# Causal attention: probabilities normalised and turned on TensorE instead of scores computed a second time transposed

## What is computed

```python
def _L3_attn_ref(x, Wk, Wq, Wv, Wp, bp):
    B, T, C = x.shape
    H = N_HEADS
    hs = C // H
    k = (x @ Wk).reshape(B, H, T, hs)
    q = (x @ Wq).reshape(B, H, T, hs)
    v = (x @ Wv).reshape(B, H, T, hs)
    scale = C ** (-0.5)
    wei = jnp.einsum('bhtd,bhsd->bhts', q, k) * scale
    mask = jnp.tril(jnp.ones((T, T), dtype=bool))
    wei = jnp.where(mask, wei, -jnp.inf)
    wei = jax.nn.softmax(wei, axis=-1)
    out = jnp.einsum('bhts,bhsd->bhtd', wei, v).reshape(B, T, C)
    return out @ Wp + bp
...
    t = t + _L3_attn_ref(_ln_t(t), L3_attn_Wk, L3_attn_Wq, L3_attn_Wv, L3_attn_Wp, L3_attn_bp)
    t = t + _L3_ffn_ref(_ln_t(t), L3_ffn_gate_w, L3_ffn_gate_b, L3_ffn_w1, L3_ffn_b1, L3_ffn_w2, L3_ffn_b2)
```

## Time and profile before

| | |
|---|---|
| runs of before (us) | 1140.48, 1141.38, 1141.67; median 1141.38 |
| profiled execution: own time, span | 1142.76, 1140.9 |
| PE, DVE, ACT, POOL busy | 91%, 59%, 51%, 45% of the span |
| causal attention's steps | about 765 to 974 us of the span |
| mean granted TensorE clock | 0.958 of full |

### The profile page before, as it was taken

One profiled execution on the slowest core, in us unless ns is written; L12 is line 12 of the kernel. 1 busy time (PEld: TensorE's weight loads), 2 busy tenths in 40 slices (PEclk: granted clock), 3 DMA queues, 4 the chain that ended last, 5 costly groups with the idle time before them and its releaser, 6 DMA issues. The chain is left out here.

```text
span 1140.9 us, 29004 instructions
## 1 busy us (share of the span) xinstructions
PE 1034.0 (91%) x11331; PEld 681.5 (60%) x11331; DVE 668.3 (59%) x1874; ACT 582.7 (51%) x1335; POOL 513.2 (45%) x675
## 2 busy tenths in 40 slices
PE   5999989799979799999999987888888888999998
PEld 2677755477745467776767754554545544466665
DVE  3899834499846456565656653774655556333333
ACT  1676633377633465666666644453444322465553
POOL 4666556487474455554545356242000000364532
PEclk9999999799989899999999997897999997899999
DMA  6500000000000000000000000000000000000000
GB/s 125 96 5 2 2 2 2 1 1 3 1 2 2 1 1 1 2 2 1 1 2 1 2 1 1 2 2 1 1 1 2 1 1 1 1 16 9 9 15 16
DMA packets 28390, 9.72 MB, mean 9 GB/s; under 512 B 26529, under 2 KB 28256, under 8 KB 28256
## 3 DMA queue, kind: packets, MB, share of 16 engines
q1 hardware_dynamic: 25232, 6.95, 2.9%
q10 hardware_dynamic: 3024, 0.92, 0.4%
HBM read 6.29 MB, written 1.57 MB: 7 GB/s over the span
## 5 line engine op out<-in xcount | busy, mean ns | idle before, releaser
L1141 POOL TENSOR_TENSOR fa_e<-fa_e,fa_rc 128x1024 f32<-128x1024 f32 x64 | 120.6, 1895 | 142.2 <-DVE fa_rc L1364 142.2
L1298 ACT ACTIVATE fa_e<-bank,fa_nm 128x256 f32<-128x256 f32 x256 | 118.9, 500 | 0.0
L164 POOL TENSOR_TENSOR ln_v<-MV,eps 128x2 f32<-128x2 f32 (+3 forms) x81 | 16.4, 203 | 162.6 <-DVE MV L201 89.7
L137 PE MATMUL bank<-hT,e_w 96*64 96x512 f32 x384 | 89.4, 600 | 0.0
L2149 ACT ACTIVATE ex_G<-bank,e_b 128x512 f32<-128x512 f32 x96 | 64.5, 687 | 47.3 <-PE bank L137 44.6
L2221 DVE SCALAR_TENSOR_TENSOR X<-bank,ex_L,X 128x96 f32<-128x96 f32 x128 | 31.7, 311 | 91.5 <-PE bank L137 85.0
L1358 DVE TENSOR_REDUCE fa_nm<-bank 128x4 f32<-128x1024 f32 x64 | 75.5, 1220 | 14.5 <-PE bank L1167 14.5
L2052 POOL TENSOR_TENSOR ex_tmp<-e_b,ex_L 128x384 f32<-128x384 f32 x8 | 6.7, 835 | 170.6 <-DVE ex_L L2209 170.6
L1871 ACT ACTIVATE ca_e<-bank 128x768 f32<-128x768 f32 x48 | 38.9, 811 | 82.0 <-PE bank L1680 82.0
L1953 DVE TENSOR_REDUCE ca_z<-bank 128x2 f32<-128x256 f32 x96 | 48.9, 552 | 50.9 <-PE bank L1680 50.9
L137 PEld LDWEIGHTS bank<-e_w,ex_G 128*64 128x64 f32 x1536 | 67.2, 137 | 17.2 <-issue 10.5
(11 more groups left out here) (253 smaller groups left out, 2500.4 us busy)
## 6 DMA issues: line engine op xcount, KB each, us to landing
out_tokens<-X SPq DMA_DIRECT2D x8, 192.0 KB, 2.1
X<-in_x SPq DMA_DIRECT2D x14, 96.0 KB, 3.4
e_w<-in_L_ffn_w SPq DMA_DIRECT2D x2, 576.0 KB
bias0r<-in_L_conv_rpb_table ACTq DMA_DIRECT2D x16, 24.0 KB
m0w<-in_L_conv_mlp_w SPq DMA_DIRECT2D x2, 144.0 KB
m1w<-in_L_conv_w SPq DMA_DIRECT2D x2, 144.0 KB
f_w<-in_L_ffn_W SPq DMA_DIRECT2D x2, 142.5 KB
mixer<-in_mixer SPq DMA_DIRECT2D x1, 256.0 KB
```

The source lines that it names most:

```text
L137: last = pe.matmul(out[columns], weights[:, columns], moving, **flags)
L1141: pool.tensor_tensor(e, e, r.broadcast_to([P, 4, TOK]), ALU.mult).then_inc(s["nrm"], 1)
L1298: last = act.activation(E[v % 4][:, i, c, :], bank[b + i][:, c * TOK:(c + 1) * TOK], ACT.Exp, bias=NM[v % 4][:, i, c:c + 1], accum_out=SU[ ...
```

## The change

Scores are computed once, with the queries on the partitions. The exponential is taken there, image by image and block by block, with the negated maximum as ScalarE's bias and the row sum as its accumulated output. VectorE inverts the sums, GpSimd multiplies the probabilities by them (`probabilities`), TensorE turns the twelve 128x128 blocks of a step in three fills of four (`turn`, into banks 5, 6 and 7), VectorE copies the fills to ET (`turned_out`), and the value product of step c-2 is done in step c. The second pair's scores of a step are issued behind the transposes of the step before. Gone are `shifted`, the transposed mask, `maxima_t`, `shift`, the column of ones, three of the four instructions of `heads_out`, and `keep_warm` in this stage. Half of the projections are copied out by VectorE. The out projection is one block of 48 passes ahead of the first pair's masks in the fifth step of a round. GpSimd normalises in halves of a round, six ahead of the steps and two in them. Two of the residual statistics move behind the last step, and the experts' first token transposes and gate use banks 4 and 5.

```diff
-    UN = 2 * H3
-    UNITS = NG * UN
+    STEPS = NG * H3
     R = TOK * H3
+    FILLS = 3
...
+    NM = [sb(f"nm{i}", [P, NJ, 2]) for i in range(2)]
+    SU = [sb(f"su{i}", [P, NJ, 2]) for i in range(2)]
+    RC = [sb(f"rc{i}", [P, NJ, 2, 1]) for i in range(2)]
     E = [sb(f"e{i}", [P, NJ, 3 * P]) for i in range(2)]
-    T1 = sb("t1", [P, TOK])
-    T2 = sb("t2", [P, TOK])
-    rc = sb("rc", [P, TOK // 32, 1])
+    ET = [sb(f"et{i}", [P, FILLS, 4 * P]) for i in range(2)]
...
+        def probabilities(u, p):
+            pool.wait_ge(s["rec"], 2 * u + p + 1)
+            images = slice(2 * p, 2 * p + 2)
+            for c in range(2):
+                e = E[u % 2][:, images, keys(c)]
+                last = pool.tensor_tensor(e, e, RC[u % 2][:, images, c, :].broadcast_to([P, 2, (c + 1) * P]), ALU.mult)
+            last.then_inc(s["nrm"], 1)
...
+        for m in range(3):
+            for i in range(2):
+                norm(m, i)
+        for u in range(STEPS):
+            for p in range(2):
+                probabilities(u, p)
+            if u in (7, 8):
+                norm(3, u - 7)
+            if u == 15:
+                next(run)
...
+        def scores(u, p):
+
+            n, h = u // H3, u % H3
+            if u == 0:
+                pe.wait_ge(s["abe"], 6)
+                if p:
+                    pe.wait_ge(s["v"], 3)
+            elif h == 0 and p == 0:
+                pe.wait_ge(s["abe"], 6 + 3 * n)
+                pe.wait_ge(s["abd"], 3 * n)
+            after(pe, s["exp"], 2 * (u - 1) + p + 1)
             for c in range(2):
+                for j in range(2 * p, 2 * p + 2):
+                    pe.matmul(bank[j][:, keys(c)], A[n % 2][strip(j, D3), cols(h, c, c + 1)], B[n % 2][strip(j, D3), cols(h, 0, c + 1)],
+                              start=(c == 0), stop=False, skip_group_check=True)
+
+        def masks(p):
+
+            for j in range(2 * p, 2 * p + 2):
+                last = pe.matmul(bank[j][:].rearrange("p (a c) -> p a c", a=2)[:, :, 0:P], k.identb[:],
+                                 k.causal[:, None, :].broadcast_to([P, 2, P]), start=False, stop=True, skip_group_check=True)
+            last.then_inc(s["sc"], 1)
...
+        def turn(u, f):
...
+            pe.wait_ge(s["nrm"], 2 * u + min(f, 1) + 1)
+            landed(u - 1, f)
...
+            if h == 4 and n >= 1:
+                pe.wait_ge(s["oc"], NJ * (n - 1) + f + 2)
+            for b in range(4):
+                j, part = divmod(4 * f + b, 3)
+                last = pe.transpose(bank[5 + f][:, b * P:(b + 1) * P], E[u % 2][:, j, part * P:(part + 1) * P], k.ident[:])
+            last.then_inc(s["et"], 1)
+
+        def landed(u, f):
+
+            if u >= 0:
+                pe.wait_ge(s["ete"], FILLS * u + f + 1)
+
+        def values(u):
...
+            landed(u, FILLS - 1)
+            after(pe, s["ote"], u)
...
+            for q in range(2):
                 for j in range(NJ):
-                    last = pe.matmul(bank[4][strip(j), c * P:TOK], V[n % 2][:, 2 * h + c, j, :], E[step % 2][:, j, 2 * c * P:(c + 2) * P],
-                                     start=(c == 0), stop=(c == 1), skip_group_check=True)
+                    last = pe.matmul(bank[4][strip(j), q * P:TOK], V[n % 2][:, 2 * h + q, j, :], turned[u % 2][:, j, 2 * q * P:(q + 2) * P],
+                                     start=(q == 0), stop=(q == 1), skip_group_check=True)
...
+        for c in range(STEPS + 2):
+            n, h = c // H3, c % H3
+            m, fetch = n + 1, n + 1 < NG
+            if 1 <= c < STEPS:
+                scores(c, 0)
+            if h == 4 and n >= 1:
+                pe.wait_ge(s["ote"], c - 2)
+                for f in range(FILLS):
+                    landed(c - 2, f)
+                if fetch:
+                    pe.wait_ge(s["abe"], 6 + 3 * n + 3)
+                    pe.wait_ge(s["abd"], 3 * n + 3)
+                out(n - 1)
+            if 1 <= c < STEPS:
+                masks(0)
+            after(pe, s["ote"], c - 2)
+            if h == 0 and fetch:
+                if c == 0:
+                    pe.wait_ge(s["v"], 3)
+                tokens(m, 0, 4)
+            elif h >= 3 and fetch:
+                if h == 4 and n >= 1:
+                    pe.wait_ge(s["oc"], NJ * (n - 1) + 1)
+                value_rows(m, h - 3, 4)
+            elif c == STEPS - 5:
+                next(run)
+            if 1 <= c <= STEPS:
+                for f in range(FILLS):
+                    turn(c - 1, f)
+            if c < STEPS:
+                scores(c, 1)
+                masks(1)
+            if h == 0 and fetch:
+                landed(c - 1, 0)
+                tokens(m, 1, 5)
+            elif h == 5 and n >= 1:
+                for half in range(2):
+                    landed(c - 1, 1 + half)
+                    out_t(n - 1, half)
+            elif h in (1, 2, 3) and fetch:
+                for i in range(2):
+                    landed(c - 1, i)
+                    project(m, 2 * (h - 1) + i, 5 + i)
+            elif c == STEPS - 4:
+                landed(c - 1, 0)
+                next(run)
+            if c >= 2:
+                values(c - 2)
...
+        def exps(u, p):
+
+            act.wait_ge(s["nm"], 2 * u + p + 1)
+            after(act, s["et"], FILLS * (u - 1))
+            after(act, s["rec"], 2 * (u - 2) + p + 1)
+            for j in range(2 * p, 2 * p + 2):
+                for c in range(2):
+                    last = act.activation(E[u % 2][:, j, keys(c)], bank[j][:, keys(c)], ACT.Exp,
+                                          bias=NM[u % 2][:, j, c:c + 1], accum_out=SU[u % 2][:, j, c:c + 1])
+            last.then_inc(s["exp"], 1)
...
+        for c in range(STEPS + 1):
+            n, h = c // H3, c % H3
+            m, fetch = n + 1, n + 1 < NG
+            if h == 4 and n >= 1:
+                out(n - 1)
+            if c < STEPS:
+                exps(c, 0)
+            if h == 0 and fetch:
+                tokens(m, 0, 4)
+                tokens(m, 1, 5)
+            elif h >= 3 and fetch:
+                value_rows(m, h - 3, 4)
+            elif c == STEPS - 5:
+                next(run)
+            if c < STEPS:
+                exps(c, 1)
+            if h in (1, 2, 3) and fetch:
+                project(m, 2 * (h - 1), 5)
...
+        def maxima(u, p):
+
+            dve.wait_ge(s["sc"], 2 * u + p + 1)
+            after(dve, s["exp"], 2 * (u - 2) + p + 1)
+            images = slice(2 * p, 2 * p + 2)
             for c in range(2):
+                last = dve.tensor_reduce(NM[u % 2][:, images, c], k.banks[:, images, keys(c)], AX.X, ALU.max, negate=True)
             last.then_inc(s["nm"], 1)
 
+        def turned_out(u, f):
+
+            dve.wait_ge(s["et"], FILLS * u + f + 1)
+            after(dve, s["av"], u - 1)
+            dve.tensor_copy(ET[u % 2][:, f, :], bank[5 + f][:]).then_inc(s["ete"], 1)
+
+        def inverse(u, p):
+
+            dve.wait_ge(s["exp"], 2 * u + p + 1)
+            after(dve, s["nrm"], 2 * (u - 2) + p + 1)
+            images = slice(2 * p, 2 * p + 2)
+            dve.reciprocal(RC[u % 2][:, images, :, 0], SU[u % 2][:, images, :]).then_inc(s["rec"], 1)
...
+        def heads_out(u):
...
+            dve.tensor_copy(OT[n % 2][:, h * TOK:(h + 1) * TOK], bank[4][:, 0:TOK]).then_inc(s["ote"], 1)
...
+        for c in range(STEPS + 3):
+            n, h = c // H3, c % H3
+            m, fetch = n + 1, n + 1 < NG
+            if c >= 3:
+                heads_out(c - 3)
+            if c < STEPS:
+                maxima(c, 0)
+                if c == 0:
+                    yield
+            if 1 <= c <= STEPS:
+                for f in range(FILLS):
+                    turned_out(c - 1, f)
+            if c < STEPS:
+                maxima(c, 1)
+            if c < STEPS:
+                inverse(c, 0)
+            if h in (1, 2, 3) and fetch:
+                project(m, 2 * (h - 1) + 1, 6)
+            elif h == 5 and n >= 1:
+                for half in range(2):
+                    residual(n - 1, half)
+            elif h in (0, 4) and n >= 2 and c < STEPS:
+                statistics(dve, k, s, 2 * (n - 2) + h // 4, 4)
+            if c < STEPS:
+                inverse(c, 1)
```

More of the change, by code:

```diff
@@ L1677, in masked @@
-        def masked(p, mask):
-            for jj in range(2):
-                last = pe.matmul(bank[2 * p + jj][:].rearrange("p (a c) -> p a c", a=2)[:, :, 0:P], k.identb[:],
-                                 mask[:, None, :].broadcast_to([P, 2, P]), start=False, stop=True, skip_group_check=True)
-            return last
-        def products(u):
-            p = u % 2
-            new, old = u < UNITS, 1 <= u <= UNITS
-            if new:
-                if u % UN == 0:
-                    pe.wait_ge(s["abe"], 6 * (u // UN + 1))
-                after(pe, s["exp"], u - 1)
-                if u // UN == NG - 1 or u % UN in (4, 5, 6):
-                    keep_warm(pe, k, bank[2 * p][:])
-            if old:
```

(52 more changed lines are left out.)

287 lines of the change are left out of this document (81 added, 206 removed).

## The result

The changed kernel takes 1155.25 us (median of 4 runs, 1152.96 to 1162.44) against 1141.11 us for the kernel before in the same session: a ratio of 1.0135, 95% interval 1.0086 to 1.0183. It is slower by some 14 us; the interval runs from 10 to 21. The profiled execution took 1157.42 us with a span of 1155.6.

What follows compares the result with a forecast made beforehand. A ring of scores, maxima, transposed maxima and shift bounds the causal attention, not TensorE. Terms: -12.6 at full clock, +6 start, +20.2 later clock falls = +13.6 on 1142.76: 1155 us; overall range 1131 to 1172.

Steps and rivals of the forecast that it cites:

- The ring: Causal attention: second-pair scores wait behind the previous step's transposes, so one turn is one step, 7.14 us at full clock.
- drain: End of the causal attention: eight transposes, the last copy and the values take 3.0 us, plus 1 at low clock.
- The quiet step of before: Earlier kernel's causal attention, last round: units follow every 3.34 us, so a quiet step of two costs 6.7 us.
- the first rival: Causal attention's quiet steps: the clock holds, giving 1134.8 us, or 1129 if the start is spared too; chance 0.25.
- Out steps: Fifth step of rounds 2, 3 and 4: out projection ahead of masks makes it 13.4 us, 12.7 in round 4.
- The start: Causal attention's first steps: VectorE's feed-forward statistics last until 771.68 us, unchanged; low clock for two steps adds 6 us.
- The clock: Causal attention: low TensorE clock adds 6 us at the start and 20.2 later, bounds 8.8 and 36.6 on the latter.
- The step that failed: Quiet steps: transposes do not count as busy for the clock, so all eleven are hit, 1.2 us each, 13.2 us.
- Its other reading: Quiet steps: if transposes held the clock, the two waits alone, 2.6 us, might spare some of the eleven steps.
- The dropped dummies: Quiet steps have no dummy matmul; in round 4 of before the clock holds, though with one in every unit.
- Fill 0: TensorE's first transposes of a step: wait until 5.3 us of the turn, when GpSimd's first-pair product ends.
- VectorE's list: Rival in the causal attention: VectorE's copies or longer signals make the step 7.6 us, clock holding: 1145 us; chance 0.08.

Runs made afterwards that it cites:

- the short products: Changed kernel with GpSimd multiplying only 32 columns of each block row instead of 128 or 256, leaving out most of the normalisation: 1127.30 us, ratio 0.9877 to before.
- the dummies in the waits: Changed kernel with extra TensorE instructions inside two waits of quiet steps: 5 and 2 matmuls 1143.31 us, or 9 and 4 transposes 1143.88 us.
- S alone: Changed kernel with TensorE issuing both pairs' scores and masks ahead of the transposes, VectorE's order kept: 1139.27 us, ratio 0.9970 to before.
- both moves: Changed kernel with both pairs' scores and masks ahead of TensorE's transposes and second-pair maxima ahead of VectorE's three copies: 1107.27 us, ratio 0.9698 to before.
- VectorE's alone: Changed kernel with only VectorE's second-pair maxima moved ahead of its three copies, TensorE's order kept: 1207.63 us, ratio 1.0578 to before.

## Why the prediction came out

The forecast was 1155.0 us, the measurement 1155.25; the sum was +13.6 us, the stage ended 13.0 later. That it is this close is luck: the interval of the measurement is 11 us wide, and several terms were off and cancelled. The ring was 2.0 us cheaper than forecast over 20 turns and the later falls 1.9; the stage began 1.6 us later, its start cost 0.8 more and its drain 0.8 more.

- **The ring** was forecast at 7.14 us and measured 7.04. Exponentials (1.73), maxima (1.0) and reciprocal were as worked out, GpSimd 1.62 for 1.65, and PE's part with its signal 2.34 for 2.36. That it is the bound at full clock is shown by the short products.
- **The quiet step of before** was read as 2 x 3.34 = 6.7 us; it is 6.83. The 1.35 us that the first rival gives as TensorE's wait is VectorE's, in the last line of the earlier trace rows. TensorE's waits are 0.96, 0.35 and 0.36 us in such a step. Nor does the clock hold through round 4 of before: it is 0.60 from 960 to 980 us. The sum did not use these.
- **Out steps** 13.4, 13.4 and 12.7 us were forecast; maxima lie 13.43, 13.42 and 12.64 us apart. The projection steps hide in the ring: 844.62 to 851.70 us is 7.08.
- **The start** was to wait for VectorE's statistics until 771.68 us, "and that is not changed". They end at 773.58. Since this moves from trace to trace without an edit, it is no cost of the change that is shown.
- **The clock** was to cost 6 at the start and 20.2 later, 1 of it in the drain. The 23 intervals between second-pair maxima exceed 7.04 us and the three out steps by 24.1 us in all: 6.8 in the first three, 17.3 in the others. These are made up otherwise than forecast. Twelve turns have no projection and no out projection, not eleven. Eight of them take 7.9 to 8.9 us (8.3 forecast), one 7.67, and three stay at 7.04: 11.6 us for 13.2. What spared the three is not shown: their waits are 1.34 and 0.29, 0.76 and 0.30, 1.33 and 0.29 us, but the turn to step 5 has 1.42 and 0.29 and was hit. Two turns with projections behind a fall (833.71 to 844.62, and 887.55 to 896.38) cost 3.9 and 1.8 for 2 each, the last out step nothing for 2. That the falls are most of the loss is shown by the dummies in the waits.
- **The reason for the falls** was half wrong. The step that failed says that four extra transposes and a wait stood ahead of each fall in before, and takes from the Trainium skill (TensorE: Matmul & The Clock Gate, Part 4: PE-mode transpose) that transposes do not count as busy for the clock the way matmuls do, so that all eleven steps are hit. The measurement decides against this here: transposes and matmuls in the same waits gave 1143.9 and 1143.3 us and the same clock. Its other reading, that the two waits are what counts and some steps might be spared, is the one that held. The number came out all the same, since fewer turns were hit but a hit cost more than the 1.2 us given (1.4 on the mean of the eight).
- **The dropped dummies** were named as a part of the danger; in before they are worth nothing (0.9994).
- **Fill 0** was said to wait for the first pair's product at 5.3 us of the ring. It waits for VectorE's copy of the heads, at about 5.7. Without effect on the sum, but it spoilt two experiments.
- **The first rival's price**, 1134.8 us with a clock that holds, was too low. With dummies in the waits most quiet turns are back at 7.04 us, and the time is 1143. What is left in that trace is 11.2 us in the first four turns, where 6 were given, and 3.3 in the turns to steps 13 and 14. Its first three turns run the same instructions as the changed kernel's, and the third takes 11.26 us there and 8.48 in the changed kernel: how long the clock stays low at the start differs between traces.
- VectorE's list, a rival at 0.08, is not the ring of the changed kernel, but it is the next one: it closes the ring as soon as TensorE's order is mended (S alone).

## What to carry to other kernels

When an instruction moves behind another on one engine, write down the ring that it closes and add up one turn; that sum held to 0.1 us for the changed kernel, and was 0.7 us short for S alone, 0.5 us long for both moves. A ring through in-order engines is opened only if every engine on it lets the next step's work go ahead: TensorE's order alone gave 16 us, VectorE's alone cost 52, both gave 48. Put dummies ahead of the wait that ends last, which the idle rows name, and only as long as the wait; behind it they are in the ring.

## What was not expected of the hardware

- f32 transposes on TensorE held the granted clock as matmuls did: 9 and 4 of them in the waits of a step gave 1.00 and 0.91 in the last rounds, the same as 5 and 2 bf16 matmuls of 512 columns, and 0.74 and 0.73 without either.
- Seven dummy matmuls in the first 1.67 us of a wait of 3.9 us did not prevent the fall behind it. They put it off, and the low time was 38 us for 41.
- The kernel before without dummies, with waits of 0.66, 0.67 and 0.90 us in a quiet step of 6.95, has 44 us of low time; the changed kernel, whose quiet steps of the last round have waits of 1.42 and 0.72, has 96 up to 1000 us. Nearly the same sum of waits goes with twice the low time.
